# Earlier first steps for the matrix-vector chain, and half of its row bounds on VectorE

## The chip, the cores and the metric

The kernel runs on one core of one Trainium2 chip. The metric is the device time of one execution in microseconds (us). Before the change the median of three runs is 2033.42 us (2031.25 to 2034.07). All rows come from one profiled execution, whose own time is 2035.73 us and whose span in the profile is 2034.5 us.

## The reference, cut to what matters

Tokens x are [2, 2048, 1024] float32. Three stages follow one another: `x += 0.5*ffn(layernorm(x))`, `x += attention(layernorm(x))`, `x += 0.5*ffn(layernorm(x))`. The attention is local, in blocks of 128 tokens, with squared-relu scores and one product with w_o. The ffn stage has a wide part and a narrow part:

```python
x_norm = layer_norm(x, in_gamma, in_beta)
thought = x_norm[:, -1, :] @ agg_w + agg_b            # last token of each batch only
for _ in range(4):
    t = layer_norm(thought, pn_gamma, pn_beta)
    t = gelu(t @ d1_w + d1_b)                          # 1024 -> 4096
    thought = thought + (t @ d2_w + d2_b)              # 4096 -> 1024
broadcast = (thought @ bc_w + bc_b)[:, None, :]
gate = sigmoid(x @ gate_w + gate_b)                    # all 4096 tokens
out = layer_norm(x + gate * broadcast)
```

The narrow part (the kernel calls it the thought) is two rows wide, so its cost is the weights: d1_w and d2_w are 16 MB each, read anew in every one of the four steps, in units of 128 x 1024 float32 (512 KB). The wide part is one product of all tokens with gate_w.

## The kernel before

One list, `PLAN`, is written by Python before anything is built, and each of the five engine programs walks it from front to back and issues its own share of each piece. So the place of a piece in `PLAN` is its place in every engine's queue, in SyncE's queue of transfers too, where a transfer that has to wait holds back all later ones.

Stage 1 begins with the fold: wk' wq is multiplied on TensorE in float32 (`("fold", "qk", j, e)`, line 1132). The first pass (j = 0) makes two rows of 128 (4 products of 128x512 for each e), the other six passes one row each (2 products for each e); the e-th piece of the first pass needs the e-th 128 rows of wq and of wk, which are just being loaded. ScalarE copies each finished row out of its bank (line 1344), squares it (line 1350), VectorE takes its largest value (line 1601), and SyncE stores it (line 928). Beside the fold stand the pieces of `gate_rows`: gate_w is loaded (line 912), VectorE finds the largest value of each of its 8 row tiles (`gate_max`, line 1577), makes a scale (lines 1613 to 1644), and ScalarE and VectorE split gate_w into two float16 parts (lines 1365 and 1650). Then come the 32 token tiles of the gate product (`plan_gate`, line 1101), with the transposes of tokens and of w_o (`turn`, `wo_turn`, line 1110) through two shared banks, then the second fold, and stages 2 and 3.

Between these pieces `with_thought` lays the steps of the thought, by a budget of time: `time_of` says how long a piece of TensorE lasts, `LIGHT`, `SHARE` and a common share say what a beat of steps costs, and a beat is laid down when the sum since the last one reaches its cost. Two weight steps make one beat. A weight step (`t_whole`, `t_whole_top`, line 1290) multiplies two units, 8 products of a 6-wide left side with 128x512 float32.

In the first of the four steps the weights come from the inputs as they are, and beside the product each of the 64 units gets a bound of its rows' size (the 32 `t_whole_top` steps): ScalarE takes the sum of absolute values of each row of both units (line 1495, two instructions each). From these bounds `t_scales` makes scales, with which `t_high` (ScalarE, line 1514) and `t_low` (VectorE, line 1936) later split units into halves that are stored and used in the other three steps. The slot of a unit is loaded again (`fetch_unit`, line 884) when TensorE has used it and, for a `t_whole_top` unit, when its bound has been found (`await_left`, line 857). In this phase 8 of 10 slots hold units, that is two beats of two steps.

## Time and profile before

| | |
|---|---|
| median of 3 runs | 2033.42 us (2031.25 to 2034.07) |
| profiled execution, its own time | 2035.73 us |
| its span | 2034.5 us |
| TensorE busy | 1958.1 us, 96% of the span |
| VectorE busy | 1262.6 us, 62% |
| ScalarE busy | 696.5 us, 34% |
| mean granted TensorE clock | 0.987 |

TensorE is busy for nearly all of the span, so what can be won by order alone is its idle time and the stretches in which its clock is granted at the lower of its two levels. A busy share over the whole span hides that ScalarE is nearly full in one stretch and VectorE in another; the views by window and the list of waits show that.

### The profile page before, as it was taken

The page shows a single profiled execution, that of the slowest core. Times are in us where ns is not written, and L with a number is a line of the kernel's source. Part 1 is how long each engine was busy: PE and PEld are TensorE (multiplying, and loading weights), DVE is VectorE, ACT ScalarE, POOL GpSimd, SP SyncE. Part 2 cuts the span into 40 slices and gives each one's busy share as a digit, 9 for nine tenths or more (in the row PEclk, how much of TensorE's full clock was granted, in tenths as well). Part 3 has the DMA queues.
Part 4 walks back from the last instruction along what each step waited for, and adds up shares of the span by engine and source line. Part 5 has one row for each costly group of instructions (what it writes and reads, how often), then busy time and mean ns, then how long its engine had stood idle before and what let it go on. Part 6 is the DMA issues. An engine that isn't in the chain of part 4 may idle for free.

```text
span 2034.5 us, 31033 instructions
## 1 busy us (share of the span) xinstructions
PE 1958.1 (96%) x12136; PEld 1036.5 (51%) x12136; DVE 1262.6 (62%) x2286; ACT 696.5 (34%) x1025; POOL 169.5 (8%) x278
## 2 busy tenths in 40 slices
PE   7998999999999999999999999999999999999997
PEld 3333444344434447665665655566655664444443
DVE  2322687324343567678787757666566637888887
ACT  1578546213223332223333122221122213444442
POOL 0000011000000010010100000000000001111111
PEclk9999999999999999999999999999999999999999
DMA  9589997889999863369979899989989966555552
GB/s 366 204 329 370 336 337 261 318 306 368 370 362 377 311 229 107 104 222 288 335 261 335 308 311 309 352 295 309 362 269 307 349 234 184 156 155 156 151 150 73
DMA packets 275216, 555.80 MB, mean 273 GB/s; under 512 B 149040, under 2 KB 149248, under 8 KB 274688
## 3 DMA queue, kind: packets, MB, share of 16 engines
q1 hardware_dynamic: 275072, 553.83, 78.5%
q8 instruction: 97, 1.59, 0.3%
q14 instruction: 47, 0.39, 0.1%
HBM read 406.93 MB, written 113.26 MB: 256 GB/s over the span
## 4 chain that ended last, share of the span: by engine, by line
PE 57%; DMA 11%; DVE 9%; SPq 2%; issue 1%; ACT 1%; POOL 1%; DVEq 0%; ACTq 0%
PE product_banks L1101 45%; PE product_banks L1136 4%; DMA thought_units<-parts_scratch 3%; PE thought_acc L1300 3%; PE product_banks L1235 2%; PE thought_acc L1290 2%; DMA gate_arena<-arena 2%; DMA thought_units<-in_d_w 2%; DVE bn_parts L1537 2%; DMA arena<-gate_scratch 1%; DMA arena<-qk_scratch 1%; SPq L1022 1%; DVE thought_units L1936 1%; SPq L884 1%; DVE arena L1713 1%
## 5 line engine op out<-in xcount | busy, mean ns | idle before, releaser
L1101 PE MATMUL product_banks<-gate_arena,arena 128*128 128x512 f16 x1536 | 353.6, 385 | 0.0
L1101 PE MATMUL product_banks<-wide_a,thought_units 128*128 128x512 f16 x1536 | 331.7, 379 | 0.0
L1101 PE MATMUL product_banks<-gate_arena,wide_a 128*128 128x256 f16 x2688 | 306.4, 275 | 9.4 <-DMA gate_arena<-arena 9.4
L1101 PE MATMUL product_banks<-wide_b,gate_arena 128*128 128x512 f16 x1344 | 299.2, 379 | 0.0
L1101 PEld LDWEIGHTS product_banks<-gate_arena,wide_a 128*128 128x128 f16 x2688 | 262.8, 99 | 57.0 <-issue 23.5
L1101 PEld LDWEIGHTS product_banks<-gate_arena,arena 128*128 128x128 f16 x1536 | 149.0, 99 | 197.8 <-issue 40.9
L1101 PEld LDWEIGHTS product_banks<-wide_a,thought_units 128*128 128x128 f16 x1536 | 150.3, 98 | 181.2
L1101 PEld LDWEIGHTS product_banks<-wide_b,gate_arena 128*128 128x128 f16 x1344 | 129.4, 98 | 157.6 <-issue 11.3
L1537 DVE BATCH_NORM_STATS2 bn_parts<-arena 128x6 f32<-128x512 f32 x256 | 164.3, 684 | 4.5
L2000 POOL TENSOR_TENSOR token_stats<-stats,minus_half 128x1 f32<-128x1 f32 x96 | 67.5, 703 | 988.0 <-DVE stats L1545 814.6
L1562 DVE SCALAR_TENSOR_TENSOR arena<-product_banks,inverse_gate,arena 128x512 f32<-128x512 f32 x64 | 47.8, 749 | 139.4 <-PE product_banks L1101 129.5
L1132 PE MATMUL product_banks<-wide_a,wide_b 128*128 128x512 f32 x256 | 120.0, 618 | 6.2 <-DMA wide_a<-in_w_attn 6.2
L2000 POOL TENSOR_TENSOR stats<-stats,minus_half 128x1 f32<-128x1 f32 x64 | 66.1, 1033 | 683.4 <-DVE stats L1545 399.3
L1438 ACT ACTIVATE gate_arena<-product_banks 128x256 f16<-128x256 f32 x128 | 41.5, 379 | 211.3 <-PE product_banks L1101 211.3
L1300 PE MATMUL thought_acc<-thought_units,thought_parts 128*6 128x512 f16 x1356 | 97.5, 381 | 5.5 <-DMA thought_units<-parts_scratch 4.9
L1444 ACT ACTIVATE arena<-product_banks 128x512 f16<-128x512 f32 x64 | 38.1, 596 | 185.7 <-PE product_banks L1101 185.7
L1415 ACT ACTIVATE arena<-arena,token_stats 128x1024 f32<-128x1024 f32 x32 | 39.5, 1236 | 178.2 <-DMA arena<-in_x 178.2
L1478 ACT ACTIVATE arena<-arena 128x512 f32<-128x512 f32 x64 | 40.4, 631 | 167.8 <-DVE arena L1562 167.8
L1691 DVE TENSOR_TENSOR arena<-arena,thought_row 128x1024 f32<-128x1024 f32 x32 | 39.1, 1221 | 83.2 <-DMA arena<-gate_scratch 83.2
L1235 PE MATMUL product_banks<-arena,key_weights 128*128 128x512 f16 x372 | 84.4, 379 | 2.9 <-DVE arena L1778 1.6
L1132 PEld LDWEIGHTS product_banks<-wide_a,wide_b 128*128 128x128 f32 x256 | 48.2, 197 | 68.0 <-issue 68.0
L1101 PE MATMUL product_banks<-gate_arena 128*128 128x256 f16 x672 | 78.1, 273 | 0.0
(221 smaller groups left out, 2365.5 us busy)
## 6 DMA issues: line engine op xcount, KB each, us to landing
thought_units<-parts_scratch SPq DMA_DIRECT2D x275, 512.0 KB, 7.8
thought_units<-in_d_w SPq DMA_DIRECT2D x174, 512.0 KB, 7.0
arena<-in_x SPq DMA_DIRECT2D x64, 512.0 KB, 9.3
parts_scratch<-thought_units SPq DMA_DIRECT2D x64, 512.0 KB, 6.1
x_scratch<-arena SPq DMA_DIRECT2D x64, 512.0 KB, 8.9
thought_row<-in_d_w SPq DMA_DIRECT2D x50, 512.0 KB, 7.2
arena<-x_scratch SPq DMA_DIRECT2D x40, 512.0 KB, 7.4
gate_scratch<-arena SPq DMA_DIRECT2D x32, 512.0 KB, 8.2
```

Of the source, the lines that this page charges most:

```text
L1101: mm = pe.matmul(bank, left(i, k), right(j, k), start=(n == 0), stop=(n == 3 * KD - 1))
L1132: mm = pe.matmul(bank_ap(key), wide_b[:, e, d * P:(d + 1) * P], wide_a[:, e, h * BANK:(h + 1) * BANK], start=(e == 0), stop=(e == KD - 1))
L1136: mm = pe.matmul(bank_ap(key), fold_parts("wv", e)[:, i, d * P:(d + 1) * P], fold_parts("wo", e)[:, j, h * BANK:(h + 1) * BANK], start=(e ...
L1235: mm = pe.matmul(bank_ap(key), weights_of(u, side)[:, i], value_parts(other)[:, j, h * BANK:(h + 1) * BANK], start=(side == n == 0), stop= ...
L1290: mm = pe.matmul(thought_acc[at:at + PARTS * B, :], values[:, pair[i][0], :], unit[:, h * BANK:(h + 1) * BANK], start=first, stop=last)
L1300: mm = pe.matmul(thought_acc[at:at + PARTS * B, :], value, unit[:, part, h * BANK:(h + 1) * BANK], start=first and part == 0, stop=last an ...
L1415: act.activation(ph_slots[u % PREP_RING], px_slots[u % PREP_RING], ACT.Identity, bias=st[:, 1:2], scale=st[:, 0:1]).then_inc(h0_made, 1)
L1438: act.activation(queries[:, query_place(n * GROUP + i), 0, e - 1:e + 1, :], made[:, i], ACT.Copy, scale=QUERY_SCALE).then_inc(q_high_made, 1)
L1478: act.activation(res, res, ACT.Sigmoid).then_inc(gated_3, 1)
L1537: dve.bn_stats(bn_parts[:, h, :], source[:, h * BANK:(h + 1) * BANK]).then_inc(own.up(), 1)
L1562: dve.scalar_tensor_tensor(out=res[:, cols], in0=bank_ap(key), scalar=inverse["gate"][:, :], in1=bias[:, cols], op0=ALU.mult, op1=ALU.add) ...
L2000: return pool.tensor_tensor(to, st[:, 2:3], minus_half[:, 0:1], ALU.pow)
```

## The change

Three things are edited. First, `time_of` gives the eight pieces of the first fold's first pass single costs (0, 2.4, 1.2, then 3.6) where each cost 1.0, so that the thought's first beats stand behind single pieces of this pass; `gate_rows` gets 8 rests ahead of its `gate_max` pieces where it had 3, and is paced at 1.0 where it was 0.9. Second, a `t_whole` step of the first matrix (agg) costs half a share. As the budget is spread over the whole of stage 1, all later beats of the first thought move too: measured in TensorE work of the main pieces, weight steps stand some 15 us earlier at first, 7 to 8 us earlier about the second fold, and in the old place at the end; the second thought is untouched. Third, the bound of the second unit of each pair is taken by VectorE (largest absolute value, a `tensor_reduce`) and no more by ScalarE, and the one semaphore `tops_found` becomes two.

```diff
--- before.py
+++ after.py
@@ -112,6 +112,7 @@
     slot: int
     turn: int
     before: tuple
+    half: int
 
 
 @dataclass
@@ -177,7 +178,8 @@
         slot = min(slots, key=lambda at: self.taken_at.get(at, -1))
         self.taken_at[slot] = n
         self.turns[slot] += 1
-        self.loads.append(Load(matrix, k, c, how, used, slot, self.turns[slot], self.take(slot, ("load", n))))
+        half = (c if matrix == "d1" else k) % 2
+        self.loads.append(Load(matrix, k, c, how, used, slot, self.turns[slot], self.take(slot, ("load", n)), half))
         return n
 
     @staticmethod
@@ -333,11 +335,17 @@
     return made + other
 
 
+
+
+FIRST_PASS = [0.0, 2.4, 1.2] + [3.6] * (KD - 3)
+
+
 def time_of(piece):
 
-
+    if piece[:3] == ("fold", "qk", 0):
+        return FIRST_PASS[piece[3]]
     if piece[0] == "fold":
-        return 1.0 if piece[1:3] == ("qk", 0) else (1.83 if piece[1] == "qk" else 1.28) * FOLD_SIZES[piece[2]]
+        return (1.83 if piece[1] == "qk" else 1.28) * FOLD_SIZES[piece[2]]
     return {"turn": 0.55, "wo_turn": 0.55, "gate": 1.71, "q": 2.67, "v": 1.71, "score": 1.75, "collect": 1.3}[piece[0]]
 
 
@@ -345,11 +353,14 @@
 
 
     beats, made, due = list(beats), [], 0.0
-    kinds = [kind for beat in beats for kind, _ in beat]
+    steps = [step for beat in beats for step in beat]
+
+    part = lambda kind, step: 0.5 if kind == "t_whole" and step.info[:1] + step.info[2:3] == (0, "agg") else SHARE.get(
+        kind, 1.0)
     times = sum(time_of(piece) for piece in main if piece[0] in PE_PIECES)
-    light = sum(LIGHT.get(kind, 0.0) for kind in kinds)
-    share = (times - light - 5.0) / sum(SHARE.get(kind, 1.0) for kind in kinds if kind not in LIGHT)
-    cost = lambda beat: sum(LIGHT.get(kind, share * SHARE.get(kind, 1.0)) for kind, _ in beat)
+    light = sum(LIGHT.get(kind, 0.0) for kind, _ in steps)
+    share = (times - light - 5.0) / sum(part(*step) for step in steps if step[0] not in LIGHT)
+    cost = lambda beat: sum(LIGHT.get(kind, share * part(kind, step)) for kind, step in beat)
     for piece in main:
         made.append(piece)
         if piece[0] in PE_PIECES:
@@ -543,14 +554,14 @@
 
 
 def whole_plan():
-    gate_rows = [("gate_rows",), ("x", 0)] + [("rest",)] * 3
+    gate_rows = [("gate_rows",), ("x", 0)] + [("rest",)] * 8
     gate_rows += [("gate_max", k) for k in range(KD)]
     gate_rows += [("scale_t", "gate"), ("rest",), ("scale_a", "gate"), ("rest",), ("scale_b", "gate")]
     gate_rows += rounded_ahead("gate", [])
     wo_ahead = 3
     gate_rows += [("x", 1), ("x", 2)] + [("wo_rows", n) for n in range(wo_ahead)] + [("norm", 0), ("rest",)]
     gate_rows += [("norm_h", 0), ("norm", 1), ("rest",), ("norm_h", 1), ("turn", 0, 0), ("turn", 0, 1)]
-    fold_qk = paced(plan_fold("qk"), gate_rows, 0.9, PE_PIECES)
+    fold_qk = paced(plan_fold("qk"), gate_rows, 1.0, PE_PIECES)
     fold_qk.append(("fold_store", "qk", KD - 1))
     wo = []
     for n in range(KD):
@@ -804,7 +815,9 @@
     h3_made, gated_3, y3_made, ended_3 = sem("h3_made"), sem("gated_3"), sem("y3_made"), sem("ended_3")
     mean3_made, squared_3 = sem("mean3_made"), sem("squared_3")
     t_pe, t_dve, t_act, t_pool = (sem(f"thought_{n}") for n in ("pe", "dve", "act", "pool"))
-    whole_used, unit_used, tops_found = sem("whole_used"), sem("unit_used"), sem("tops_found")
+    whole_used, unit_used = sem("whole_used"), sem("unit_used")
+
+    tops_found = [sem("tops_found_act"), sem("tops_found_dve")]
     unit_high, unit_low = sem("unit_high"), sem("unit_low")
     act_own_sem, dve_own_sem, pool_own_sem = sem("act_own"), sem("dve_own"), sem("pool_own")
 
@@ -854,7 +867,7 @@
         elif LOADS[n].how in ("whole", "top"):
             eng.wait_ge(whole_used, LOADS[n].used + 1)
             if LOADS[n].how == "top":
-                eng.wait_ge(tops_found, LOADS[n].used - KD // 2 + 1)
+                eng.wait_ge(tops_found[LOADS[n].half], LOADS[n].used - KD // 2 + 1)
         elif LOADS[n].how == "pair":
             eng.wait_ge(unit_used, LOADS[n].used + 1)
         else:
@@ -1489,16 +1502,11 @@
             elif kind == "t_whole_top":
 
                 _, both, matrix, pair, *_ = a[0].info
-                for half in range(2):
-                    at = scaled_at(matrix, *pair[half])
-                    await_unit(act, both[half])
-                    top = act.activation(parts_at(FOR_SPLITS[half])[:, 0], unit_at(LOADS[both[half]].slot), ACT.Abs,
-                                         accum_out=unit_scale[:, at:at + 1])
-                    if half == 0:
-                        top.then_inc(own.up(), 1)
-                        act.wait_ge(own.sem, own.n)
-                    else:
-                        top.then_inc(tops_found, 1)
+                at = scaled_at(matrix, *pair[0])
+                await_unit(act, both[0])
+                act.wait_ge(tops_found[0], a[0].tops)
+                act.activation(parts_at(FOR_SPLITS[0])[:, 0], unit_at(LOADS[both[0]].slot), ACT.Abs,
+                               accum_out=unit_scale[:, at:at + 1]).then_inc(tops_found[0], 1)
             elif kind == "t_high":
                 _, n = a[0].info
                 split = SPLITS[n]
@@ -1888,10 +1896,17 @@
                         dve.wait_ge(own.sem, own.n)
                     else:
                         made.then_inc(t_dve, 1)
+            elif kind == "t_whole_top":
+                _, both, matrix, pair, *_ = a[0].info
+                at = scaled_at(matrix, *pair[1])
+                await_unit(dve, both[1])
+                dve.tensor_reduce(unit_scale[:, at:at + 1], unit_at(LOADS[both[1]].slot), AX_X, ALU.max,
+                                  apply_absolute_value=True).then_inc(tops_found[1], 1)
             elif kind == "t_scales":
                 t, = a
                 scale, exponent = unit_scale[:, :], unit_inverse[:, :]
-                dve.wait_ge(tops_found, t.tops)
+                for found in tops_found:
+                    dve.wait_ge(found, t.tops)
                 dve.tensor_scalar(scale, scale, TINY, None, ALU.max).then_inc(own.up(), 1)
                 dve.wait_ge(own.sem, own.n)
                 dve.tensor_scalar(exponent.bitcast(I32), scale.bitcast(I32), EXPONENT_BITS, None,
```

VectorE, from the first `t_mean` (L1860 before, L1868 in the change) on. Before; `scale_stat_gate` is `gate_max`, `scale_stat_qk` a finished fold row:

```order
L1860 TENSOR_REDUCE t_small<-thought_turn 128x2
L1863 TENSOR_SCALAR centred<-thought,t_small 128x8 x2
L1866 TENSOR_TENSOR squares<-centred 128x16
L1577 TENSOR_REDUCE scale_stat_gate<-arena 128x1
L1601 TENSOR_REDUCE scale_stat_qk<-arena 128x1 x2
L1577 TENSOR_REDUCE scale_stat_gate<-arena 128x1
L1872 TENSOR_REDUCE t_small<-thought_turn 128x2
L1874 TENSOR_SCALAR t_small<-t_small 128x2
L1878 TENSOR_SCALAR thought<-centred,t_small 128x8 x2
L1577 TENSOR_REDUCE scale_stat_gate<-arena 128x1
```

The same place in the change:

```order
L1868 TENSOR_REDUCE t_small<-thought_turn 128x2
L1871 TENSOR_SCALAR centred<-thought,t_small 128x8 x2
L1874 TENSOR_TENSOR squares<-centred 128x16
L1880 TENSOR_REDUCE t_small<-thought_turn 128x2
L1882 TENSOR_SCALAR t_small<-t_small 128x2
L1886 TENSOR_SCALAR thought<-centred,t_small 128x8 x2
L1868 TENSOR_REDUCE t_small<-thought_turn 128x2
```

No reduction of gate_w and none of a fold row stands any more between the first norm's two halves; the first of them now follows the thought's first product.

TensorE at the program's start, before (L1132 is the fold, 4 rows of it are one piece of the first pass; L1264 and L1270 are thought steps):

```order
L1132 MATMUL product_banks<-wide_a,wide_b 128x512 x8
L1264 MATMUL thought_turn<-identity,t_wide 128x128
L1132 MATMUL product_banks<-wide_a,wide_b 128x512 x4
L1270 MATMUL thought_turn<-thought,mean_maker 128x16
L1132 MATMUL product_banks<-wide_a,wide_b 128x512 x14
L1270 MATMUL thought_turn<-squares,mean_maker 128x16
```

And in the change (L1145 is the fold, L1303 the first weight steps):

```order
L1283 MATMUL thought_turn<-thought,mean_maker 128x16
L1145 MATMUL product_banks<-wide_a,wide_b 128x512 x4
L1283 MATMUL thought_turn<-squares,mean_maker 128x16
L1145 MATMUL product_banks<-wide_a,wide_b 128x512 x4
L1283 MATMUL thought_turn<-thought,mean_maker 128x16
L1145 MATMUL product_banks<-wide_a,wide_b 128x512 x4
L1283 MATMUL thought_turn<-squares,mean_maker 128x16
L1145 MATMUL product_banks<-wide_a,wide_b 128x512 x4
L1303 MATMUL thought_acc<-thought_units,narrow_in 6x512 x8
```

Both norms now lie within the first pass, with one piece of it between any two steps, and the first weight steps directly behind it.

ScalarE about the end of the first fold, before (L1495 is a unit's bound, L1344 and L1350 are a fold row, L1328 the transposed tokens, L1373 the transposed w_o):

```order
L1495 ACTIVATE thought_units,unit_scale<-thought_row 128x1024 x2
L1495 ACTIVATE thought_units,unit_scale<-thought_units 128x1024 x2
L1344 ACTIVATE arena<-product_banks 128x512 x2
L1350 ACTIVATE thought_units,scale_stat_norm<-arena 128x1024
L1495 ACTIVATE thought_units,unit_scale<-thought_units 128x1024 x4
L1328 ACTIVATE arena<-turn_banks 128x512 x2
L1373 COPY wide_a<-turn_banks 128x4x128
```

The same place in the change:

```order
L1508 ACTIVATE thought_units,unit_scale<-thought_row 128x1024
L1508 ACTIVATE thought_units,unit_scale<-thought_units 128x1024
L1357 ACTIVATE arena<-product_banks 128x512 x2
L1363 ACTIVATE thought_units,scale_stat_norm<-arena 128x1024
L1341 ACTIVATE arena<-turn_banks 128x512 x2
L1508 ACTIVATE thought_units,unit_scale<-thought_units 128x1024 x2
L1386 COPY wide_a<-turn_banks 128x4x128 x2
```

Ahead of the tokens' transposes no bound stands any more behind the last fold row, and there are two for each beat where there were four.

## Rows read from the trace of the kernel before

**Rows 1.** The page, part 2: the span in 40 slices.

```profile
DVE  2322687324343567678787757666566637888887
ACT  1578546213223332223333122221122213444442
```

**Rows 2.** Who TensorE waited for, 6 to 230 us: us, times, longest.

```profile
PE turn_banks L1110 <- DVE arena L1554: 4.8, 3, 3.2
...
PE thought_acc L1290 <- DMA thought_units<-in_d_w: 2.3, 2, 1.6
PE turn_banks L1110 <- ACT wide_a L1373: 1.6, 2, 1.4
PE thought_acc L1290 <- DMA thought_row<-in_d_w: 1.3, 1, 1.3
```

**Rows 3.** Busy time by window: PE, PEld, DVE, ACT, POOL, granted clock, DMA share, GB/s.

```profile
40.00:60.00 20.00, 16.43 (x49) 6.50 (x49) 15.12 (x26) 2.48 (x6) 1.41 (x2) 0.91 0.63 245
...
120.00:140.00 20.00, 17.11 (x62) 5.80 (x61) 2.99 (x10) 11.95 (x22) 0.74 (x2) 0.91 1.02 401
...
160.00:180.00 20.00, 16.77 (x97) 6.40 (x90) 4.54 (x9) 18.00 (x32) 0.73 (x2) 0.91 0.91 347
...
260.00:280.00 20.00, 16.18 (x83) 7.04 (x80) 16.36 (x28) 9.50 (x11) 1.46 (x4) 0.91 0.84 306
40.00:230.00 190.00, 176.16 (x780) 70.56 (x780) 69.18 (x149) 121.07 (x202) 7.19 (x16) 0.96 0.83 306
```

**Rows 4.** VectorE in order of time, 39 to 47 us: start, us, ..., [idle before].

```profile
43.62 1.21 DVE L1577 TENSOR_REDUCE scale_stat_gate<-arena 128x1 f32<-128x1024 f32 x1
44.74 0.17 DVE L1872 TENSOR_REDUCE t_small<-thought_turn 128x2 f32<-128x16 f32 x1
```

**Rows 5.** TensorE in order of time, 40 to 230 us.

```profile
46.56 0.40 PE L1270 MATMUL thought_turn<-thought,mean_maker 128*128 128x16 f32 x2 [3.57 <-DVE thought L1878]
46.80 5.38 PE L1132 MATMUL product_banks<-wide_a,wide_b 128*128 128x512 f32 x8
...
70.69 3.60 PE L1132 MATMUL product_banks<-wide_a,wide_b 128*128 128x512 f32 x8
```

**Rows 6.** TensorE's weight loads in order of time, 26 to 34 us.

```profile
26.04 0.19 PEld L1270 LDWEIGHTS thought_turn<-thought,mean_maker 128*128 128x128 f32 x1 [0.24 <-issue]
...
26.58 0.30 PEld L1132 LDWEIGHTS product_banks<-wide_a,wide_b 128*128 128x128 f32 x2
...
30.07 0.30 PEld L1132 LDWEIGHTS product_banks<-wide_a,wide_b 128*128 128x128 f32 x2 [0.61 <-issue]
...
33.91 0.19 PEld L1132 LDWEIGHTS product_banks<-wide_a,wide_b 128*128 128x128 f32 x1 [0.97 <-issue]
```

**Rows 7.** Groups by line, 60 to 210 us, ScalarE.

```profile
L1495 ACT ACTIVATE thought_units<-thought_units 128x1024 f16<-128x1024 f32 x48 | 50.4, 1050 | 1.2 <-DMA thought_units<-in_d_w 0.4
```

**Rows 8.** Groups by line, 30 to 210 us, VectorE.

```profile
L1577 DVE TENSOR_REDUCE scale_stat_gate<-arena 128x1 f32<-128x1024 f32 x8 | 9.4, 1211 | 12.6 <-DMA arena<-in_gate_w 12.6
```

**Rows 9.** Who the queue of transfers waited for, 40 to 230 us.

```profile
SPq L857 <- ACT thought_units L1495: 89.1, 28, 15.2
```

**Rows 10.** ScalarE in order of time, 157 to 167 us (the first of four bounds).

```profile
160.74 1.06 ACT L1495 ACTIVATE thought_units<-thought_units 128x1024 f16<-128x1024 f32 x1
...
165.19 1.06 ACT L1328 ACTIVATE arena<-turn_banks 128x512 f16<-128x512 f32 x2
```

**Rows 11.** Who TensorE waited for, 230 to 730 us.

```profile
PE turn_banks L1110 <- DVE scale_stat_wv L1608: 3.8, 1, 3.8
...
PE thought_turn L1308 <- DVE t_wide L1943: 3.2, 1, 3.2
PE product_banks L1136 <- DVE arena L1562: 2.5, 1, 2.5
```

**Rows 12.** Transfers issued from 35 to 60 us: count, KB each, us to landing.

```profile
thought_units<-in_d_w SPq DMA_DIRECT2D x4, 512.0 KB, 5.5
qk_scratch<-arena SPq DMA_DIRECT2D x2, 512.0 KB, 15.0
```

## The prediction

> **What bounds the kernel now.** The page comes first: TensorE is busy 96% of the span, so its work bounds the kernel, and this change neither adds nor removes products. What an order can win is idle time and clock. The 40 slices [rows 1] show where: in slices 3 to 4 (about 100 to 200 us) ScalarE is full (8, 5, 4, 6 tenths and near them, against 1 to 3 later), and VectorE is light there (2 to 4). Next, the list of who TensorE waited for, cut to 6 to 230 us [rows 2], where nearly all the edits lie: 4.8 us for transposes behind VectorE, 1.6 us behind ScalarE, 2.3 and 1.3 us for weight units in flight, and one wait of 3.57 us that the order of time shows [rows 5]. The windows [rows 3] add the clock: granted at 0.91 over 40 to 60, 120 to 140 and 160 to 180 us, and 0.96 over 40 to 230. A window of 20 us at 0.91 has lost 20 x 0.09 = 1.8 us to the lower level (1.2 of 2.4 GHz); each follows a wait (the first at once: 8 products take 5.38 us behind the 3.57 us wait and 3.60 us at 70.69, a difference of 1.78 [rows 5]). 190 x 0.04 = 7.6 us makes about four such falls. So a wait costs itself and, where the clock falls behind it, 1.8 us more.
>
> **Part A, the first pass.** The wait of 3.57 us ends with VectorE's `thought` (line 1878). VectorE could read the norm's second sum (line 1872) only at 44.74, since two `gate_max` and two fold rows stood ahead of it in its queue, and the first of these waited for its row of gate_w (the 12.6 us of [rows 8]); the last of them began at 43.62 [rows 4]. In the changed order neither stands between the steps of the two norms: each step has one piece of the first pass (3.6 us of TensorE) behind it, and the chain from one step to the next (about 1.8 us from 44.74 to 46.56 [rows 4, 5]) fits under it. So the wait and the fall of clock behind it go: 3.57 + 1.78 = 5.35 us. What is late next here is a weight piece: the weight loads of the last pieces start after gaps of 0.61 and 0.97 us where 0.24 is usual [rows 6], 1.1 us in which the pass waits for wq and wk. Three more small steps move into this pass; one costs 26.58 - 26.04 = 0.54 us [rows 6], 1.6 us for three, of which 1.1 us fill the gaps. Since they are missing later, the gain is 1.1 us. Part A gives 6.4 us, between 3.6 (the clock falls elsewhere) and 6.4.
>
> **Part B, the bounds of the units.** 64 units have a bound, 32 `t_whole_top` steps of two. On ScalarE one takes 1.05 us and a read of 0.19 that partly overlaps; the four from 160.74 to 165.19 take 1.11 us each [rows 7, 10]. 32 of them leave ScalarE: 36 us. VectorE takes them as a reduction of 128x1024 float32; the same operation on a tile of the same shape is `gate_max` with 1.21 us [rows 8], so 32 x 1.21 = 39 us go onto VectorE. It is busy 2.99 and 4.54 of 20 us in the windows where they land [rows 3], and so hides them; without that cover each in front of a transpose or a bank would cost up to its 1.21 us, 39 us in all, which is the far bound. The Trainium skill ("VectorE: DVE Perf Modes", section "Rules for kernel authors") warns of exactly this operation: on a hot path it runs at the plain rate, is the slowest of this engine, and one should restructure. By that rule the move is a bad trade; by the rows a reduction costs within a tenth of what ScalarE pays, on an engine with room, and the sum stays.
>
> The use of it is the latency. The transfer queue waited 89.1 us in 28 waits for ScalarE's bounds [rows 9]: a slot is free only when both bounds of its step are in. For a beat of two steps ScalarE needs 4 x 1.11 = 4.4 us, half of it after the change, with the other half beside it on VectorE, so the reload of a slot is asked for some 2.2 us earlier, and more where ScalarE has a backlog. The unit waits that this should remove are 2.3 + 1.3 us in three waits [rows 2] and one fall of clock, 1.8 [rows 3]: 5.4 us together. I take all of it; the bounds are 0 (the transfers are at a share of 1.02 in that window [rows 3] and cannot come faster) and 5.4.
>
> The other use is the queue on ScalarE. From 160.74 to 165.19 four bounds stand ahead of the copies of the tokens' transposes at 165.19 [rows 10], and TensorE waits for the bank (the longest of the 4.8 us, 3.2 [rows 2]). In the changed order two bounds stand ahead of the last fold row and none between it and the copies, and later beats have two where there were four. Such waits to 230 us are 4.8 + 1.6 us [rows 2], with two falls of clock, 3.6: 10.0 us in all. By the order of `PLAN`, 28 of the 32 `t_whole_top` steps stand ahead of the gate's first tile, where 22 stood, so fewer bounds stand among transposes. I take 6 of the 10; the bounds are 0 and 10.
>
> **Part C, what is moved past other things.** The two stores of the first fold rows stood ahead of the thought's reloads on the transfer queue and now stand behind 8 of them. A store issued in the full queue took 15.0 us to land, a unit in an emptier one 5.5 [rows 12]. ScalarE needs the first store for the third fold row, which TensorE ends about 20 us after the first pass: 8 x 0.524 MB at the 401 GB/s of a full window [rows 3] are 10.5 us of transfers in front, on top of the 15.0, and ScalarE may start the row some 5 us late (an estimate). TensorE needs that bank only two fold rows later, 14 us, which hides it; but the first bounds and reloads slide by up to 3 us. Price 0 to 3 us. The Trainium skill ("DMA: Bandwidth & Descriptors", section "Anatomy of one DMA — SWDGE (gpsimd) path") says that transfer engines never wait on a semaphore, the issuing sequencer does; by that rule everything behind a waiting reload waits too, and the 89.1 us of waits [rows 9] are of that kind.
>
> New waits also come from the new neighbours of every later beat: a bound on VectorE behind a fold row, a half (`t_low`) among the maxima of wv and wo. I take 4 us for all of part C, two waits of 1 us and one fall of clock with the rest; bounds 0 and, from the rows below, 15.
>
> **Beyond 230 us.** Beats stand 7 to 14 us earlier against the gate's tiles, so the waits there change company: 3.8 us behind a scale of wv (in a window with VectorE busy 16.36 of 20 us and clock 0.91 [rows 3]), 3.2 and 2.5 us [rows 11], 9.5 us, and with three falls of clock about 15. Each comes from VectorE being full, and no work leaves VectorE there. I take zero with bounds of 8 either way. From about 500 us on the order is as it was.
>
> **The sum.** 6.4 + 5.4 + 6 - 4 = 13.8 us off the profiled execution's 2035.73: 2021.9. That execution is 2.3 us above the median, so I predict 2033.4 - 13.8 = 2020 us (rounded).
>
> **Rivals.** First, transfers still gate the units: only part A is won, and part B's unit waits merely move. For it: shares of 1.02 and 0.91 in [rows 3]. Against it: a share of 0.83 over 40 to 230 us and 0.63 from 40 to 60, holes that earlier reloads fill. Part A less 1 us of stores: 2033.4 - 5.4 = 2028.
>
> Second, what is won early is given back later: stage 1 is bound by volume and by VectorE from 160 us on, and the 14 us come back as waits at 230 to 400 us, where beats now meet other work. For it: VectorE at 16.36 of 20. Against it: TensorE's order fixes its work, and only a wait as long as the gain returns it. 2033.
>
> Third, slower: VectorE's queue becomes the wait. Place: the gate's tiles from 160 to 400 us, where VectorE drains transposes and banks, stands behind a bound or a half whose unit is late, and TensorE waits. Price: each such wait is like the one of 3.8 us [rows 11] with its fall of clock, 5.6 us. The point from which it decides is four of them, 22 us, more than the 13.8; with four 2033.4 - 13.8 + 22 = 2042. For it: that row. Against it: only the last 4 of the 32 new reductions stand among the gate's tiles, in windows with VectorE at 3 to 5 of 20 us.
>
> **How the numbers follow.** The forecast 0.66, transfers 0.15, given back 0.11, slower 0.08. The forecast's own range is 2012 (all 10 of the queue waits, and 4 of those beyond 230 us) to 2028. With the rivals, and leaving out less than 2 in 10, the range is 2010 to 2033. A measurement of this kernel can tell about 0.2%, 4 us, from none: faster is under 2029.3. The forecast gives nearly all of its 0.66 and the transfers 0.13: faster 0.79. Within: the given-back case and edges, 0.13. Slower: 0.08.
>
> **What would show it.** TensorE's wait before `t_mean` at 43 us gone and the clock there at 1.00; the first weight steps (line 1303) at about 38 us, directly behind the first pass. The transfer queue's waits for ScalarE's bounds (89.1 us) at less than half, with VectorE's beside them. Windows 120 to 180 us without a granted clock of 0.91, ScalarE's share there down by a third. Reductions of 1.2 us on VectorE. The prediction is wrong if new waits of over 2 us on transposes appear between 150 and 400 us, if units are waited for as before, or if the early gain is there at 230 us and gone at 500.

## The result, and the profile after

The changed kernel takes 2012.51 us (median of 4 runs, 2010.06 to 2017.0), the kernel before on the same chip 2032.34 (4 runs, 2025.26 to 2034.07): a ratio of 0.9909, 95% interval 0.9888 to 0.993. A second series of the same kernel gave 0.9915 (0.989 to 0.994, 5 runs). By these ratios the change is faster by some 18 us, known to about 4; 13.8 were predicted. The profiled execution took 2012.83 us with a span of 2011.6, against 2034.5 before: 22.9 us.

The page of the changed kernel first, its engines and two rows of the 40 slices:

```profile
PE 1945.9 (97%) x12136; PEld 1034.9 (51%) x12136; DVE 1300.5 (65%) x2318; ACT 661.9 (33%) x961; POOL 166.4 (8%) x278
...
DVE  2666687224444566677887766766566638888887
ACT  1455455213232323223433212222112213444442
```

Against [rows 1], ScalarE's 5, 7, 8, 5 in the second to fifth slice are 4, 5, 5, 4, and VectorE's 3, 2, 2 in the second to fourth are 6, 6, 6. The work moved as the diff says, and TensorE's share rose because the same products lie in a shorter span.

The windows of the changed kernel (us, PE, PEld, DVE, ACT, POOL, granted clock, DMA share, GB/s):

```profile
40.00:60.00 20.00, 20.00 (x68) 8.76 (x65) 9.86 (x22) 0.84 (x2) 0.69 (x1) 1.00 1.03 408
60.00:80.00 20.00, 18.02 (x75) 5.82 (x74) 12.10 (x16) 9.13 (x16) 0.00 (x0) 0.91 0.63 220
120.00:140.00 20.00, 20.00 (x79) 7.09 (x81) 9.54 (x13) 11.82 (x20) 0.74 (x2) 1.00 0.86 319
160.00:180.00 20.00, 18.31 (x114) 8.63 (x112) 12.57 (x24) 13.00 (x21) 0.73 (x2) 1.00 1.02 411
260.00:280.00 20.00, 20.00 (x112) 9.30 (x114) 17.79 (x30) 10.12 (x12) 3.01 (x4) 1.00 0.96 346
340.00:360.00 20.00, 17.17 (x91) 6.37 (x92) 7.82 (x7) 4.29 (x4) 0.00 (x0) 0.91 0.80 281
560.00:580.00 20.00, 13.80 (x85) 5.49 (x83) 7.40 (x15) 5.13 (x7) 0.73 (x2) 0.96 1.03 411
580.00:600.00 20.00, 20.00 (x110) 9.16 (x111) 9.79 (x19) 7.16 (x10) 1.70 (x2) 0.87 0.96 356
40.00:230.00 190.00, 181.93 (x847) 75.65 (x844) 112.07 (x176) 95.20 (x148) 7.81 (x14) 0.99 0.92 348
```

Beside [rows 3]: the windows at 40, 120, 160 and 260 us, all at 0.91 before, are at 1.00. TensorE is busy 181.93 of the 190 us from 40 to 230, where it was 176.16, at 0.99 and not 0.96. DMA carries 348 GB/s there, not 306: the holes in the transfers were filled. Two falls of the clock were not forecast at their places: one at 60 to 80, and one spread over the last two windows of 20 us (20 x 0.04 + 20 x 0.13 = 3.4 us, twice the usual 1.8).

TensorE's waits in the changed kernel, 6 to 230 us (engine, line, what it waited for: us, times, longest), which answer to [rows 2]:

```profile
PE turn_banks L1123 <- DVE arena L1562: 4.7, 3, 2.3
PE turn_banks L1160 <- DVE scale_stat_gate L1621: 2.0, 1, 2.0
PE thought_acc L1303 <- DMA thought_units<-in_d_w: 0.9, 1, 0.9
PE turn_banks L1123 <- ACT wide_a L1386: 0.5, 2, 0.2
```

The 3.57 us wait of [rows 5] is gone, the units cost 0.9 us where they cost 3.6, the transposes 5.2 where they cost 6.4, and a wait of 2.0 us on gate_w's maximum is new. Of the 4.7 us behind VectorE, 2.3 are one wait at 227 us; before the change no wait for a transpose from 200 to 240 us was over 1.1 us. From 230 to 730 us, to be held against [rows 11]:

```profile
PE turn_banks L1123 <- ACT arena L1403: 9.6, 3, 6.2
PE product_banks L1149 <- DVE arena L1570: 4.4, 1, 4.4
PE thought_turn L1321 <- DVE t_wide L1958: 2.9, 1, 2.9
PE thought_acc L1313 <- DVE thought_parts L1944: 2.0, 1, 2.0
PE turn_banks L1123 <- DVE scale_stat_wv L1616: 1.5, 1, 1.5
```

[rows 11] begins with the third line of its view. The two above it, before the change, are these:

```profile
PE thought_acc L1300 <- DVE thought_parts L1929: 4.3, 1, 4.3
PE turn_banks L1110 <- ACT arena L1390: 4.2, 2, 3.2
```

The waits met other company: 4.3 us on the thought's parts became 2.0, 3.8 on the scale of wv became 1.5, and a wait of 6.2 us for a transpose behind ScalarE is new. And the queue of transfers, 40 to 230 us, beside the 89.1 us of [rows 9]:

```profile
SPq L870 <- ACT thought_units L1508: 49.4, 12, 16.8
...
SPq L870 <- DVE unit_scale L1903: 7.7, 6, 3.0
```

Two sums give the whole of it. Over the whole span TensorE's listed waits add up to 65.0 us before and 54.3 after, 10.7 less. The clock lost 2034.5 x 0.013 = 26.4 us before and 2011.6 x 0.007 = 14.1 after, 12.3 less. Together they make 23.0 of the 22.9 us, so about half of the gain between these two profiles is clock (a granted clock is rounded to 0.001, 2 us). That is more than in the other runs. The 56 runs of the kernel before that stand beside the experiments have a mean of 2029.7 us and 0.9893, the nine runs of the changed kernel 2013.0 and 0.9920: 2029.7 x 0.0107 - 2013.0 x 0.0080 = 5.6 of 16.7 us, a third.

Where it came can be read by finding the same product of the main work in both traces. The one at 269.20 us before stands at 256.03 after (13.2 us won); 357.69 at 342.83 (14.9); 556.9 at 542.5 (14.4); 597.73 at 579.84 (17.9, behind the wait of 6.2 us); 846.57 at 827.92 (18.7). At the first three places the changed kernel has also made 16 products of the thought more, since its beats stand earlier, so a little more is won there than the place says. From 597.73 and 579.84 on both have made the same products, 896 of the thought and 1899 of the rest.

By waits and falls instead of places: to 230 us, leaving out the wait for the first transfers at 6 us, the waits fell from 14.4 to 8.6 us and four falls of the clock became one, 5.8 + 3 x 1.7 = 11 us. From 230 to 850 us the waits fell from 26.0 to 21.7 and six falls, a double one counted as two, became four: 4.3 + 3.4 = 7.7. Nearly 4 us, to 22.9, come after that, where the order is the same, and are mostly two late falls; the experiments show that these are not the change's.

### The profile page after: what moved, and what is told of

Read it like the earlier page. It is cut to its first block, busy times and chain, and to the rows that moved or that the text cites. A ratio compares the mean times of both kernels' runs of the same rounds, so it can differ in the third digit from the quotient of the medians.

```text
span 2011.6 us, 30999 instructions
## 1 busy us (share of the span) xinstructions
PE 1945.9 (97%) x12136; PEld 1034.9 (51%) x12136; DVE 1300.5 (65%) x2318; ACT 661.9 (33%) x961; POOL 166.4 (8%) x278
## 4 chain that ended last, share of the span: by engine, by line
PE 57%; DMA 10%; DVE 9%; SPq 3%; ACT 2%; issue 2%; POOL 1%; DVEq 0%; ACTq 0%
PE product_banks L1114 45%; PE product_banks L1149 4%; PE thought_acc L1313 3%; PE product_banks L1248 2%; DMA arena<-qk_scratch 2%; DMA thought_units<-parts_scratch 2%; DMA arena<-gate_scratch 2%; PE thought_acc L1303 2%; DVE bn_parts L1545 2%; DMA thought_units<-in_d_w 2%; SPq L1035 2%; DVE thought_units L1951 1%; SPq L897 1%; DVE arena L1721 1%; PE turn_banks L1123 1%
## 5 line engine op out<-in xcount | busy, mean ns | idle before, releaser
L1114 PE MATMUL product_banks<-gate_arena,arena 128*128 128x512 f16 x1536 | 347.1, 380 | 0.0
L1145 PE MATMUL product_banks<-wide_a,wide_b 128*128 128x512 f32 x256 | 121.2, 620 | 5.8 <-DMA wide_a<-in_w_attn 5.8
L1145 PEld LDWEIGHTS product_banks<-wide_a,wide_b 128*128 128x128 f32 x256 | 48.0, 196 | 68.1 <-issue 68.1
```

The costliest lines, as they stand in the source:

```text
L1114: mm = pe.matmul(bank, left(i, k), right(j, k), start=(n == 0), stop=(n == 3 * KD - 1))
L1145: mm = pe.matmul(bank_ap(key), wide_b[:, e, d * P:(d + 1) * P], wide_a[:, e, h * BANK:(h + 1) * BANK], start=(e == 0), stop=(e == KD - 1))
```

## The experiments

The theory is the prediction's: the gain to 230 us comes from the first pass (part A) and from the bounds (part B), each for itself. The rivals are that the order alone does it, through transfers or the clock, and that the surprises (the wait at 71 us, the one at 579 us) are new costs of the change that hide more of the gain. Ratios are to runs of the kernel before on the same chip.

**The bounds alone.** The order of before; the second bound on VectorE:

```
+            elif kind == "t_whole_top":            # VectorE
+                dve.tensor_reduce(unit_scale[:, at:at + 1], unit_at(LOADS[both[1]].slot), AX_X, ALU.max, ...)
```

> Only the second bound of each pair moves to VectorE; the order of PLAN is that of before. My theory (the two edits win apart: the order wins in the first 60 us and by fewer bounds among transposes, the bounds win by shorter queues on ScalarE): the wait of 3.57 us at 43 us stays, unit waits (3.6 us to 230 us) fall under 1 us, transposes' waits (6.4 us) fall to 3, two or three of the four falls of clock to 230 us go: 8 us faster, 2024. Rival (the order alone wins, VectorE's bounds are worth nothing because TensorE was there only held by the places of the beats): within 2 us of before, 2031. Second rival (VectorE's queue, full at 200 to 360 us, now holds TensorE): 2036.

Measured: 2024.23 us (10 runs), ratio 0.9974 (0.9963 to 0.9985). Its order of time at TensorE shows what stays:

```profile
47.03 0.61 PE L1274 MATMUL thought_turn<-thought,mean_maker 128*128 128x16 f32 x2 [3.57 <-DVE thought L1877]
47.48 5.43 PE L1136 MATMUL product_banks<-wide_a,wide_b 128*128 128x512 f32 x6
```

The wait of 3.57 us is there to the digit, and the clock in the window 40 to 60 us is 0.83, a double fall where the kernel before had a single one. Its transfer queue waited 60.9 us for ScalarE, not 89.1. The bounds are worth 5.3 us. Its waits, 6 to 230 us, and a window:

```profile
PE turn_banks L1114 <- DVE arena L1553: 3.7, 4, 1.1
...
PE thought_acc L1294 <- DMA thought_units<-in_d_w: 2.0, 2, 1.5
PE turn_banks L1114 <- ACT wide_a L1377: 0.5, 2, 0.2
```
```profile
160.00:180.00 20.00, 17.12 (x106) 6.45 (x106) 11.35 (x15) 12.52 (x21) 0.73 (x2) 1.00 0.97 374
```

In the old order, with half of the bounds gone from ScalarE, the waits for transposes are 4.2 us where they were 6.4, the longest 1.1 and not 3.2, and the windows 120 to 200 us, three of which were at 0.91, are all at 1.00.

**The order alone.** The changed order; both bounds stay on ScalarE.

> The changed order of PLAN, but ScalarE takes both bounds of each step as before. My theory: the wait at 43 us and its fall of clock go (5.4 us), weight steps lie in the first pass (1.1 us), but the transfer queue waits for ScalarE as long as before (some 80 to 90 us) and the unit waits of 2 to 4 us with a fall of clock stay, and the late first store (ScalarE held to 63 us) makes them worse, since 4 bounds follow: 8 us faster than before, 2024. Rival (all comes from the order): as the whole change, 2013. If ScalarE held to 63 us decides: 2030.

Measured: 2017.76 us (6 runs), ratio 0.9940 (0.9926 to 0.9954), 12.2 us. Waits, 6 to 230 us:

```profile
PE turn_banks L1121 <- DVE arena L1565: 4.7, 3, 2.3
PE thought_acc L1301 <- DMA thought_units<-in_d_w: 3.2, 2, 2.4
```

Units are waited for 3.2 us here and 0.9 in the change, and the transfer queue waits 80.0 us for ScalarE. That fits part B, in which the bounds' use is the latency of the reloads. The waits for transposes behind VectorE are 4.7 us, and 0.5 behind ScalarE, to the digit what the change has, with the windows 120 to 200 us at 1.00 too. So the waits of 160 to 190 us and their falls go by either edit: by fewer bounds in the queue (the bounds alone), or by beats that stand elsewhere. The two medians add up, 5.3 + 12.2 = 17.5 where the change gave 18, though this term can be won only once. Where the bounds win on top of the order isn't seen in the waits: over the whole profile they are 53.9 us here, 54.3 in the change and 50.6 in its control below.

**Stores first.** In the change, the stores of the first two fold rows stand ahead of the last piece of the first pass:

```
+            if (m, j, e) == ("qk", 0, KD - 1):
+                out.extend(("fold_store", m, i) for i in range(FOLD_SIZES[0]))
             out.append(("fold", m, j, e))
-            if e == 4 and j:
+            if e == 4 and j > (m == "qk"):
```

> The whole change, and the stores of the first two fold rows stand in the transfer queue ahead of the thought's first 8 reloads again. My theory (the first store behind 8 reloads held ScalarE 22.4 us to 63 us, VectorE's bounds and maxima came late behind it, and TensorE waited 1.98 us at 71 us with a fall of clock of 1.7): that wait and the fall go, 3.7 us faster than the change, 2009. Rival (the maxima of gate_w on VectorE are late whatever ScalarE does): the wait stays, 2012.5. Rival (the units now land later by the two stores, and a unit is waited for at 62 us): 2 us slower, 2014.5.

Measured: 2011.06 us (5 runs), ratio 0.9913 (0.9899 to 0.9928); the change itself 0.9909 and 0.9915. Why it was tried, in the trace of the changed kernel, SyncE's queue, ScalarE, VectorE and TensorE in order of time:

```profile
47.87 2.12 SPq L941 DMA_DIRECT2D qk_scratch<-arena  x2
```
```profile
63.27 1.08 ACT L1357 ACTIVATE arena<-product_banks 128x512 f32<-128x512 f32 x2 [22.42 <-DMA qk_scratch<-arena]
```
```profile
64.45 1.22 DVE L1609 TENSOR_REDUCE scale_stat_qk<-arena 128x1 f32<-128x1024 f32 x1 [6.02 <-ACT arena L1357]
65.59 3.46 DVE L1585 TENSOR_REDUCE scale_stat_gate<-arena 128x1 f32<-128x1024 f32 x3
68.97 2.33 DVE L1903 TENSOR_REDUCE unit_scale<-thought_units 128x1 f32<-128x1024 f32 x2
```
```profile
71.43 0.38 PE L1160 MATMUL turn_banks<-scale_stat_gate,mean_maker 128*128 128x1 f32 x2 [1.98 <-DVE scale_stat_gate L1621]
71.67 4.11 PE L1145 MATMUL product_banks<-wide_a,wide_b 128*128 128x512 f32 x6
```

The stores, issued at 47.87 us behind eight reloads, held ScalarE for 22.4 us; the third fold row came late; VectorE, which takes its queue in order, did gate_w's maxima and two bounds behind it; TensorE waited 1.98 us and its clock fell. With the stores first this wait and the fall are gone: the window 60 to 80 us is at 1.00 and its DMA carries 309 GB/s, not 220. That is 3.7 us in a profile, yet the ratios of the two kernels are the same. Their intervals leave room for at most some 4 us, and these runs can't tell that from none.

**Rests alone.** The kernel before with 8 rests and not 3 in `gate_rows`.

> The kernel before with one edit: 8 rests where 3 stood ahead of the maxima of gate_w. The thought's beats keep their places. My theory (the wait at 43 us is VectorE's queue, two maxima and two fold rows ahead of the norm's sum): the wait and its fall of clock go, 5 us faster, 2027, if the later scale and rounding of gate_w do not hold anything. Rival (the wait belongs to the thought's late place in the first pass, and another wait takes its place): 2031 to 2033.

Measured: 2028.38 us (12 runs), ratio 0.9989 (0.9977 to 1.0002): no difference that is clear of noise. Its waits, 6 to 230 us:

```profile
PE turn_banks L1110 <- DVE arena L1554: 7.5, 4, 4.2
...
PE turn_banks L1110 <- ACT wide_a L1373: 2.5, 2, 2.3
PE thought_acc L1290 <- DMA thought_units<-in_d_w: 1.3, 1, 1.3
```

The wait at 43 us is gone, and the transposes cost 10.0 us where they cost 6.4. This is the danger behind part A: a wait was removed by moving work off it, and another place waited longer. That the moved maxima made the longer waits fits the rows but was not followed back.

**The change once more**, as a control.

> The whole change once more, beside the others on one chip, so that it can be compared with them, and to see whether its profile again has no fall of clock after 950 us, where the kernels before, with one bound moved, and with the order alone all had two (at about 1130 and 1495 us). My theory (stages 2 and 3 have the same order in all of these, and these falls come and go from run to run): 18 us faster than before, with a fall of clock at 1100 or 1480 us in some profiles. Rival (the early start also smooths the last stages): 22 us faster and again none.

Measured: 2013.35 us (5 runs), ratio 0.9915 (0.989 to 0.994). It shows what differs with no edit at all, here 1480 to 1500 us, the second run and then the first:

```profile
1480.00:1500.00 20.00, 17.46 (x150) 12.53 (x149) 11.71 (x24) 2.44 (x5) 1.51 (x5) 0.91 1.05 339
```
```profile
1480.00:1500.00 20.00, 17.25 (x150) 11.78 (x148) 10.24 (x20) 2.44 (x5) 1.46 (x4) 1.00 1.07 341
```

Same kernel, the same work in the window, and the clock at 0.91 in one and 1.00 in the other. TensorE is idle for 2.5 us of this window in the one and for 2.8 in the other. Of the two late falls before the change the control has this one; the order alone has both (0.91 at 1120 to 1140 and at 1480 to 1500 us). So late falls that are missing in the changed kernel's profile are chance and not the order. The wait before the transposes at 579 us is in both runs (6.20 and 6.17 us): that one is the order's.

**Both bounds on VectorE.**

```
-                at = scaled_at(matrix, *pair[1])          # the second unit
+                for half in range(2):                     # both, ScalarE none
+                    at = scaled_at(matrix, *pair[half])
```

> The whole change, but VectorE takes both bounds of each step and ScalarE none. My theory (what the moved bounds win is that two engines share a beat's four bounds; a queue of four on VectorE is as long as one of four on ScalarE, and VectorE also drains the transposes): the gain of moving the bounds, 5 us, is lost, and transposes wait for VectorE between 150 and 200 us: 5 to 8 us slower than the change, 2018. Rival (it is only ScalarE that must be free): as the change or better, 2011. It leaves out nothing.

Measured: 2018.74 us (10 runs), ratio 0.9950 (0.9933 to 0.9968), some 7 us slower than the change. Waits, 6 to 400 us:

```profile
PE product_banks L1149 <- DVE arena L1562: 4.4, 1, 4.4
PE thought_turn L1321 <- DVE t_wide L1951: 4.2, 2, 2.5
PE turn_banks L1160 <- DVE scale_stat_gate L1613: 4.0, 1, 4.0
```

The wait at 71 us doubles from 1.98 to 4.0 us, and the transfer queue waits 79.7 us for VectorE's bounds. This is the mechanism of the prediction's third rival, at 71 us and not among the gate's tiles: VectorE's queue, already the wait of 2 us there with 32 reductions, is 4 us with 64. Over the whole profile the waits are only 2.2 us more than in the control (52.8 and 50.6), and the granted clock is 0.990 and not 0.992, 4 us, so more of this price is clock than wait.

**Sides sooner.** Stores first, and the work beside the early gate tiles paced at 1.0 and not 0.9:

```
-    early += paced([p for n in range(5, EARLY) for p in plan_gate(n)], sides, 0.9, PE_PIECES)
+    early += paced([p for n in range(5, EARLY) for p in plan_gate(n)], sides, 1.0, PE_PIECES)
```

> The change with the two stores first, and the splits of wv and wo paced at 1.0 where it is 0.9, so that VectorE's last halves of wo lie ahead of gate tile 11 and not beside its bank. My theory (the wait of 4.44 us at 343 us and its fall of clock are VectorE's queue of two wo halves and two thought halves ahead of the last bank of the gate): the wait falls to under 2 us and the fall goes, 4 us faster, 2007; the cost is a denser VectorE at 250 to 300 us, whose waits of 1.5 and 2.9 us may grow. Rival (a wait only moves): 2011.

Measured: 2007.93 us (5 runs), ratio 0.9897 (0.9868 to 0.9926), 3 us under the stores first (0.9913), which is within the intervals.

```profile
PE product_banks L1151 <- DVE arena L1572: 1.4, 1, 1.4
```

The wait of 4.4 us at 343 us is 1.4 and its fall is gone, the others are 3.2 and 2.0. But three new falls stand at 223, 253 and 291 us (0.91 in each of these windows, where the change has 1.00), and the kernel with all three mends below has the same three. So the use of this edit isn't shown by itself.

**Rows ahead.** Stores first, and in `rounded_ahead` for qk and vo a finished row is split and its successor fetched before the next one is rounded:

```
-        out += ([("round", m, k + 1)] if k + 1 < KD else []) + [("split", m, k)] + fetches[k:k + 1]
+        after = [("round", m, k + 1)] if k + 1 < KD else []
+        out += [("split", m, k)] + fetches[k:k + 1] + after if fetches else after + [("split", m, k)]
```

> The change with the two stores first, and each row of the folded weights is fetched 5 pieces of TensorE ahead of its rounding on ScalarE, where it was 2. My theory (at 566 to 577 us ScalarE stands 11.4 us in a rounding whose row is still in flight, the token norm behind it is late, and TensorE waits 6.2 us with a fall of clock of twice the usual length): ScalarE's waits for such rows (31 us in 4) fall under 5 us, TensorE's wait there goes: 8 us faster, 2003. Rival (the rows come no earlier, since the transfers are at a share near 1.0 there): 2009 to 2011.

Measured: 2004.07 us (5 runs), ratio 0.9868 (0.9843 to 0.9893). The reason, from the changed kernel, TensorE and ScalarE in order of time, and ScalarE's waits from 500 to 640 us:

```profile
579.84 1.11 PE L1123 MATMUL turn_banks<-identity,arena 128*128 128x128 f32 x4 [6.20 <-ACT arena L1403]
```
```profile
577.50 1.15 ACT L1378 ACTIVATE wide_a<-arena,scale_stat_qk 128x1024 f16<-128x1024 f32 x1 [11.38 <-DMA arena<-qk_scratch]
```
```profile
ACT wide_a L1378 <- DMA arena<-qk_scratch: 31.3, 4, 11.4
```

TensorE waits for ScalarE, but ScalarE stands in its queue before a rounding whose row of wk' wq is still in flight. Fetched earlier, in the kernel with the rows ahead:

```profile
ACT wide_a L1381 <- DMA arena<-qk_scratch: 9.8, 2, 6.5
```

There TensorE's waits from 400 to 850 us are 8.2 us, not 13.6 as with the stores first alone, the windows 560 to 600 us are at 1.00, and the time is 9 us less.

**All three mends** (stores, sides, rows).

> The change with all three mends: stores first, splits of wv and wo at a pace of 1.0, rows fetched 5 pieces ahead of their rounding. My theory (each mend takes away its own wait, and the waits are apart in time: 71 us, 343 us, 578 us): the rows' mend gives 8 us over the stores', the splits' 3 to 4 more: 2001, 12 us faster than the change. Rival (the splits' mend did nothing beyond noise, since the clock fell at three new places between 220 and 290 us): 2004, as with two mends.

Measured: 1997.36 us (4 runs, 1995.78 to 1997.65), ratio 0.9835 (0.9821 to 0.985). It beats the kernel before by 33 us and the change by some 15.

**The costs of the first pass alone.** The kernel before with `FIRST_PASS`; 3 rests, pace 0.9, full shares, bounds on ScalarE.

> The kernel before with the single costs of the first pass alone (0, 2.4, 1.2, then 3.6): the maxima of gate_w keep 3 rests and pace 0.9, agg keeps its full share, ScalarE takes both bounds. My theory (the gain of the order lies in the thought's earlier beats, in the first pass and by fewer bounds among the gate's transposes; the rests add nothing that the earlier norm steps do not already have): the wait at 43 us goes, and most of the 12 us of the order edit come, 10 us faster than before, 2020. Rival (a maximum of gate_w, whose row lands late, now stands ahead of a fold row and of the sum of agg on VectorE and holds TensorE there): 4 us faster, 2026.

Measured: 2013.89 us (6 runs), ratio 0.9922 (0.9906 to 0.9938): within the intervals as much as all three edits, with every bound on ScalarE, and no worse than the order alone (0.9940), which holds the rests and the half share too. So one list of eight costs does most of what the change does. Its VectorE and TensorE in order of time:

```profile
64.16 1.22 DVE L1605 TENSOR_REDUCE scale_stat_qk<-arena 128x1 f32<-128x1024 f32 x1 [8.29 <-ACT arena L1348]
65.30 0.17 DVE L1864 TENSOR_REDUCE t_small<-thought_turn 128x2 f32<-128x16 f32 x1
...
65.89 0.17 DVE L1870 TENSOR_TENSOR squares<-centred 128x16 f32<-128x16 f32 x1
```
```profile
66.12 0.61 PE L1274 MATMUL thought_turn<-squares,mean_maker 128*128 128x16 f32 x2 [6.26 <-DVE squares L1870]
```

The late stores hold ScalarE here too (22.5 us), and now the norm's squares stand behind the late fold row: 6.26 us and a double fall (0.83 from 60 to 80 us). In return there is no wait of 6.2 us at 579: the window 560 to 580 is at 1.00. It has one large wait at another place. With all bounds on ScalarE its waits for transposes to 230 us are 3.4 us and those for units 1.0, and no window from 120 to 200 us is under 1.00.

**The change with a full share for agg.**

```
-    part = lambda kind, step: 0.5 if kind == "t_whole" and step.info[:1] + step.info[2:3] == (0, "agg") else SHARE.get(
+    part = lambda kind, step: SHARE.get(
```

> This is the change with one part taken back: a t_whole step of agg costs a full share again; the costs of the first pass, the 8 rests, the pace of 1.0 and the bounds on VectorE stay. The kernel before with the costs of the first pass alone had no wait of 6.2 us behind ScalarE at about 577 us and ran in 0.9922; the change has that wait, with a fall of the clock of double length. Theory one (the half share moves the beats behind the fourth tile of the q and k product, and so makes this wait): the wait of over 5 us at about 577 us is gone, TensorE's waits from 400 to 850 us fall from some 20 us to 10 or less, and the time is 5 to 8 us under the change, 2006 to 2009 us where the kernel before runs in 2030, ratio about 0.989. Theory two (the wait hangs on the fetching of the qk rows and not on where the beats stand): the wait is there with 4 to 7 us and the time is within 3 us of the change, ratio 0.991 to 0.993. Rival: the half share had a use early on, and without it the unit waits of 2 to 4 us before 230 us are back; then the time is 2013 to 2017, ratio 0.992 to 0.994.

Measured: 2013.2 us (5 runs), ratio 0.9922 (0.9908 to 0.9936). Its waits, 6 to 230 us and then 400 to 850 us:

```profile
PE thought_turn L1283 <- DVE squares L1874: 5.9, 1, 5.9
```
```profile
PE turn_banks L1123 <- ACT arena L1403: 6.3, 3, 3.3
```

Theory one was right about the place: the wait of 6.2 us at 579 us is 1.9, the three waits of this kind to 850 us are 6.3 us where the change has 9.6, and the windows 560 to 600 us are at 1.00. It was wrong about the time, since 5.9 us behind the late fold row came at 65 us, with the deepest fall of these kernels (0.74 from 60 to 80). So the half share has an early use (it puts the norm's squares at 52 us, ahead of the late row) and a late price, of about one size. It has a second use: the wait for the scale of wv is 4.1 us at 263 us here, with the clock at 0.91, as in the bounds alone, the rests alone and the first pass alone, and 1.5 us without a fall in the change and its control.

**The three mends with a full share.**

> The change with the three mends (stores of the first two fold rows first, the side work at pace 1.0, the qk rows fetched ahead), and with a full share for a t_whole step of agg. In the three mends the wait at 577 us is gone already, so theory one (the half share's only price is this wait) expects no further gain: ratio 0.982 to 0.985, 1995 to 2000 us where the kernel before runs in 2030, TensorE's waits from 400 to 850 us as in the three mends within 3 us. Theory two (each place of the beats has its own waits, and this one was mended for the half share): new waits of 2 to 5 us come up between 230 and 850 us, ratio 0.985 to 0.989, 2000 to 2008 us. If the ratio is under 0.982 the half share costs something in itself, which neither theory has.

Measured: 1996.1 us (5 runs, 1987.51 to 1999.58), ratio 0.9844 (0.9827 to 0.9861), as with the half share (0.9835). With the stores first nothing is late at 65 us, with the rows ahead nothing at 579, and the half share makes no difference any more that these runs can tell.

## Why the prediction was right, by its steps

The total came out a few us over the forecast and for reasons that are in part not its own. Parts A to C put all 13.8 us ahead of 230 us; 11 were won there, and 7.7 between 230 and 850 us, where the prediction had zero.

**Part A (6.4 us): right.** The wait of 3.57 us and its fall went. The bounds alone kept both, the changed order took both away. The term isn't proven as a price: with the rests alone the same wait went, and only 2 us were won, not clear of noise. (The last 1.1 us of the term were not measured apart.) What the prediction didn't see is that this holds only as long as the norm's steps stand ahead of the third fold row: in two other kernels the same norm waited 5.9 and 6.26 us.

**Part B, latency (5.4 us): right in size, the mechanism fits.** Measured in the whole change 2.7 us of unit waits (3.6 to 0.9) and a fall, 4.5. With the bounds alone the queue waited less for ScalarE (60.9 us), and unit waits were 2.0. But the first pass alone has 1.0 with every bound on ScalarE, so earlier beats do the same. The bounds alone are worth 5.3 us in the medians, and that holds this term and the next. A reduction took 1212 ns, the 1.21 us taken from `gate_max`. With 32 the reductions mostly hid and with 64 they no longer did. The warning of the Trainium skill ("VectorE: DVE Perf Modes", section "Rules for kernel authors") on this operation on a hot path fits the second case and not the first.

**Part B, queue on ScalarE (6 us): right in size, by two causes of which one is enough.** Waits for transposes fell from 6.4 to 5.2 us, and the two falls behind them went: 1.2 + 3.6 = 4.8, most of it clock. The prediction named both the fewer bounds and the moved beats and added them up as one. The bounds alone bring the waits to 4.2 us and take both falls away; the order alone, with all bounds on ScalarE, brings them to 5.2 and takes them away too.

**Part C (-4 us): the size right, the step failed.** The price was 1.98 + 1.7 = 3.7 us in the profile, though with the stores first the runs were no faster. The prediction saw the late stores and hid them behind 14 us in which TensorE doesn't need the bank. The bank was indeed no wait. It overlooked VectorE, whose queue stands behind the fold row: the delay went round by ScalarE, VectorE and gate_w's maximum to the PE. A slack must be sought on every queue that the late instruction is in.

**Beyond 230 us (0, bounds of 8): the term failed in size, some 8 us were won.** "Each comes from VectorE being full, and no work leaves VectorE there" didn't keep the waits as they were: 3.8 us on the scale of wv became 1.5, and 4.3 us on the thought's parts, which the prediction's list of three leaves out, became 2.0. The falls of the clock behind the waits at 268 and 320 us of before have no match after; those at 357 and 716 us are the ones at 341 and 696 after; the double one at 559 is gone and another stands at 577. The two at 268 and 320 us stand in both other kernels with the old order (the bounds alone, the rests alone: 0.91 in the windows 260 to 280 and 300 to 320 us), so their going is the order's. The double one isn't as sure, since those two kernels have a single one there. The wait of 6.2 us at 579 us is the one thing given back, the second rival's mechanism later than it said; it didn't turn the gain, which is 14.4 us ahead of it and 17.9 behind it. Of the last 4 us, two late falls (1142 and 1507 us before) make 3.6, and the experiments show them to be chance. The prediction also has the order as it was from about 500 us on; it is so from 598 us (580 after) on.

**The clock.** The prediction gave it 1.8 us for each of four falls in front of 230 us, and one was left there. In all it is half of the gain between the two profiles and a third of it over all runs. **The rivals:** transfers did not gate (348 GB/s where 306 were); VectorE's queue was a wait of 2 us with 32 reductions, at one place and behind a late ScalarE, and of 4 us with 64.

**A reading and the signs.** The prediction reads ScalarE as full in slices 3 to 4 by "8, 5, 4, 6"; those are slices 4 to 7 of [rows 1], and slices 3 and 4 have 7 and 8. It changes no term. Of its signs, the wait at 43 us, the first weight steps at 38.25 us, the clock from 120 to 180 us and the reductions came as said. Two fell short: the queue's waits for ScalarE went to 49.4 us, just over half of 89.1, and ScalarE's busy time from 120 to 180 us went from 46.3 to 35.9 us, by a fifth and not a third. And one of its signs of being wrong came: a new wait of over 2 us on a transpose between 150 and 400 us, the 2.3 us at 227. The order alone has it too (2.29 us), so it is the price of moved beats.

Open is which beats help between 230 and 598 us. The half share accounts for the wait on the scale of wv; the first pass alone has no fall at 300 to 320 us (1.00 in that window), so the one there goes without the half share. The waits further on were not taken apart, and neither is where the bounds win 5 us on top of the order.

## What to carry to other kernels

In a kernel whose busiest engine is at 96%, look for the wait with its fall of clock, remove it, and then look where the moved work waits now: rests alone gained nothing clear of noise, and the edit that won most was followed by one wait of 6 us wherever the beats were put. Follow such a wait back past the engine that it names until a transfer stands there; both that were left here were transfers issued too late in program order, and issuing them sooner, with one change of pace, was worth 15 us where the whole change was worth 18 (the rows of wk' wq fetched ahead were 9 of it; the stores and the pace weren't clear of noise by themselves). Move work to an engine only as far as its queue takes it: 32 reductions helped, 64 cost 7 us against that.

## What the hardware showed that was not expected

A fall behind the same wait comes in one run and not in the next (the window 1480 to 1500 us above). Five runs of the last kernel took 1987.51 to 1999.58 us, and their granted clocks are 0.997 and 0.991 at the ends: 0.006 x 1990 = 12 us, the whole spread. So two falls (3.6 us) between two profiles show nothing by themselves.

A fall comes in several sizes. In the kernel before a window of 20 us stood mostly at 0.91 behind waits of 2 to 4 us (1.8 us lost), but at 0.83 behind the 4.3 us at 561. Behind the waits of 6.2, 6.26 and 5.9 us of three other kernels 3.4 us or more were lost (0.96 and 0.87; 0.83; 0.74 in the windows concerned). The length of the wait doesn't fix it: the bounds alone showed 0.83 behind a wait of 3.57 us, where the kernel before had 0.91 behind the same wait.
